# A graph and memory-lookup network on one core: the lookup's vector y kept in PSUM, score tiles copied to SBUF, the selection spread over half steps, and layer-2 products summed over two source tiles

## The reference

```python
x = x + gelu(batch_norm(gcn(LN(x)))) + LN(x)       # layer 1, graph
y = LN(x)                                          # layer 1, lookup
q = (y @ Wq + bq).reshape(-1, 8, 128)              # 8 heads, two halves of 64
s1, s2 = q[..., :64] @ keys1.T, q[..., 64:] @ keys2.T      # 256 scores each
t1, i1 = top_k(s1, 8); t2, i2 = top_k(s2, 8)
best8, pos = top_k(all 64 sums t1[a] + t2[b], 8)
rows = i1[pos // 8] * 256 + i2[pos % 8]            # 64 rows of 65536 per node
inner = sum_d y[d] * w_down[rows, d]
x = x + sum_rows relu(inner) * softmax(best8) * w_up[rows]
x = x + (segment_sum(LN(x)*deg_out**-.5)[src] -> dst) * deg_in**-.5 @ W + b   # layer 2, graph
x = x + LN(x) @ W[bin(LN(x)[0])]                   # layer 2, one of 8 experts
```

## Time and profile before

| | µs |
|---|---|
| median of three runs | 1503.99 |
| the profiled execution, its own time | 1505.18 |
| its span, first to last instruction | 1503.4 |
| first gather issued | 369.1 |
| lookup result added: tile 0, tile 8, tile 9 | 501.35, 1269.47, 1350.38 |
| mean granted TensorE clock, share of full | 0.934 |

### The profile page before, as it was taken

One profiled execution on the slowest core, in us unless ns is written; L12 is line 12 of the kernel. 1 busy time (PEld: TensorE's weight loads), 2 busy tenths in 40 slices (PEclk: granted clock), 3 DMA queues, 4 the chain that ended last, 5 costly groups with the idle time before them and its releaser, 6 DMA issues.

```text
span 1503.4 us, 15734 instructions
## 1 busy us (share of the span) xinstructions
PE 1208.2 (80%) x3844; PEld 576.9 (38%) x3845; DVE 988.0 (66%) x2819; ACT 431.9 (29%) x1128; POOL 710.4 (47%) x706
## 2 busy tenths in 40 slices
PE   2887889975789789778887898788989897689387
PEld 1343345543434244343342443434435342234133
DVE  3778791126587977949859689497795985565411
ACT  1767610023323232322322323123232232220010
POOL 2000000001676676756767767576676677643212
PEclk9999999986798999989999999899999999899689
DMA  8200000001998999989989999899999999977343
GB/s 351 114 0 1 1 1 0 0 0 36 352 341 294 350 364 326 361 318 329 357 308 359 374 330 348 319 346 376 326 365 354 334 365 360 375 280 255 128 162 114
DMA packets 105763, 378.73 MB, mean 252 GB/s; under 512 B 11824, under 2 KB 11826, under 8 KB 104536
## 3 DMA queue, kind: packets, MB, share of 16 engines
q0 software_dynamic: 94720, 343.40, 62.0%
q1 hardware_dynamic: 10968, 34.48, 6.2%
HBM read 359.53 MB, written 19.41 MB: 252 GB/s over the span
## 4 chain that ended last, share of the span: by engine, by line
PE 44%; DVE 29%; issue 10%; DVEq 4%; another core or an unknown queue 4%; DMA 3%; ACT 3%; POOL 3%; ACTq 0%; POOLq 0%; SPq 0%
PE tr L1288 16%; DVE big L991 12%; PE acc L1190 6%; PE acc L1162 5%; PE acc L1248 4%; DVE topi L885 4%; PE acc L1266 4%; DVE top L882 3%; PE tr L1337 3%; PE tr L1313 2%; PE acc L1220 2%; POOL big L473 2%; DVE outT L876 1%; DVE outT L739 1%
## 5 line engine op out<-in xcount | busy, mean ns | idle before, releaser
L473 POOL DMA_INDIRECT big<-in_wdu,idx x640 | 664.7, 1039 | 666.3 <-DVE idx L930 359.2
L1288 PE MATMUL tr<-big,diag 128*128 128x512 f32 x1280 | 626.9, 620 | 123.2 <-ACT diag L643 66.0
L991 DVE CUSTOM_DVE_ANT_0 big<-big,y,prob 128x512 f32<-128x512 f32 x640 | 450.1, 746 | 59.3 <-DMA big<-in_wdu,idx 39.1
L1288 PEld LDWEIGHTS tr<-big,diag 128*128 128x128 f32 x1280 | 234.4, 194 | 436.6 <-issue 323.7
L643 ACT ACTIVATE diag<-ident,inner 128x128 f32<-128x128 f32 x640 | 219.4, 393 | 491.3 <-DVE inner L991 270.9
L1162 PE MATMUL acc<-outT 128*128 128x512 f16 (+1 forms) x612 | 129.4, 370 | 29.5 <-DVE outT L739 22.7
L1266 PE MATMUL acc<-AT,gt 128*128 128x512 f32 (+1 forms) x240 | 109.6, 543 | 23.8 <-DVE outT L876 13.4
L882 DVE MAX8 top<-acc 128x8 f32<-128x256 f32 x160 | 60.9, 422 | 99.5 <-PE acc L1258 50.8
L739 DVE TENSOR_SCALAR outT<-big 128x1280 f16<-128x1280 f16 x204 | 102.6, 549 | 35.2 <-PE acc L1162 33.4
L876 DVE TENSOR_TENSOR outT<-outT,acc 128x512 f32<-128x512 f32 (+1 forms) x120 | 69.9, 584 | 67.6 <-remote 45.2
L1248 PEld LDWEIGHTS acc<-yT,qk 128*128 128x128 f32 x640 | 87.4, 213 | 34.4 <-issue 33.3
(11 more groups left out here) (212 smaller groups left out, 735.0 us busy)
## 6 DMA issues: line engine op xcount, KB each, us to landing
sorted_rows<-big SPq DMA_DIRECT2D x8, 1280.0 KB, 17.3
big<-in_wdu,idx POOLq DMA_INDIRECT x640
big<-in_we SPq DMA_DIRECT2D x8, 1024.0 KB, 13.9
x<-sorted_rows SPq DMA_DIRECT2D x14, 512.5 KB, 3.4
x<-in_x SPq DMA_DIRECT2D x1, 2304.0 KB
qk<-in_wq SPq DMA_DIRECT2D x1, 2048.0 KB, 19.8
big<-in_w0t SPq DMA_DIRECT2D x1, 1024.0 KB, 27.2
qk<-in_keys SPq DMA_DIRECT2D x1, 1024.0 KB, 19.6
```

Of the source, the lines that this page charges most:

```text
L473: pool.indirect_dma_start(out=k.big[:, slot * 2 * D:(slot + 1) * 2 * D], out_offset=None, in_=k.wdu_d, in_offset=bass.IndirectOffsetOnAxis ...
L991: ins = dve.tensor_tensor_reduce(out=k.big[:, slot:slot + D], in0=k.big[:, slot:slot + D], in1=k.y[:, (i % 3) * D:(i % 3 + 1) * D], scale= ...
L1288: ins = pe.matmul(k.O[i % 2], k.diag[:, c:c + P], k.big[:, slot:slot + D], start=(g == 0 and s == 0), stop=(g == NG - 1 and s == GS - 1))
```

## The change

- **y.** VectorE computes only the factor and the offset (y_inv, two small operations); ScalarE applies them (y_norm, 128x512) into one SBUF tile, which TensorE transposes, and shortly before the tile's lookup copies it into a PSUM bank (keep_y; k.Y, two banks). The dots read y from there. Before each tile VectorE waits for `y_kept`. x_norm of layer 2 goes to ScalarE in the same way, into three h1 tiles.
- **Scores.** TensorE writes both halves of a head into one buffer of two banks; ScalarE copies them to SBUF in one instruction (copy_scores); MAX8 and FIND_INDEX8 read there. TensorE waits for ScalarE's copy of the head before. ScalarE's copy waits until the head before the last is selected. qT holds 4 heads.
- **Places.** The search of a tile starts 26 groups ahead of the one before it and takes 3 groups per head; MAX8 and FIND_INDEX8 are steps of their own (maxes, finds), and so is `sums`, taken out of best. Tile 1 has its own table. The tables below give, in this order, the places of y_stats, y_root, y_inv, y_norm, y_flip, y_copy, y_keep, the four queries, the eight scores, s_copy, maxes, finds and sums; q_copy is one place behind its query, and best, place, codes, match, rows and index follow sums one by one, softmax 8 behind it.
- **Units.** Source tiles (0,1), (2,3), (4,5), (6,7) are multiplied together: two products accumulate in the bank, then one addition; tiles 8 and 9 stay single. A unit comes every 5 groups (single ones every group). The first pair's results are copied into agg1, so the memsets go. The self-loops are subtracted before the batch norm.

```diff
-Y_STATS, Y_NORM = -14, -11
-HEADS = (-4, -3, -1, 0, 2, 3, 5, 6)
-BEST, PLACE, CODES, MATCH, ROWS, INDEX, SOFTMAX = 8, 9, 10, 11, 12, 13, 15
-Y_ROOT, Y_FLIP, Y_COPY = -13, -10, -9
-QUERIES = (-9, -7, -5, -3)
-Q_COPY = (-8, -6, -4, -2)
-SCORES = (-6, -5, -3, -2, 0, 1, 3, 4)
-X_ADD, X_STATS, X_ROOT, X_NORM = 4, 5, 6, 7
-UNIT_MM = [8 + 2 * u for u in range(NU)]
-UNIT_ADD = [11 + 2 * u for u in range(NU)]
+STEADY = Places(-26, -25, -23, -22, -21, -20, 2, (-19, -16, -9, -3), [3 * h - 15 for h in range(H)],
+                [3 * h - 13 for h in range(H)], [3 * h - 9 for h in range(H)], [3 * h - 8 for h in range(H)], 14)
+FIRST = Places(-6, -5, -4, -3, -2, -1, 1, (0, 2, 6, 8), [2 * h + 2 for h in range(H)],
+               [2 * h + 3 for h in range(H)], [2 * h + 4 for h in range(H)], [2 * h + 4 for h in range(H)], 19)
+X_ADD, X_STATS, X_ROOT, X_INV, X_NORM = 5, 8, 9, 11, 12
+UNIT_TILES = [(0, 1), (2, 3), (4, 5), (6, 7), (8,), (9,)]
+PAIRED, AHEAD = 4, 4
+for p_ in range(PAIRED):
+    for u_ in range(NU):
+        if p_ < PAIRED - 1 or u_ < AHEAD:
+            m_, a_ = (2 * p_ + 2) * NG + 14 + 5 * u_, 5
+        else:
+            m_, a_ = (NT - 1) * NG + 2 * (u_ - AHEAD), 3
+for u_ in range(NU):
+    m_ = (NT - 1) * NG + 16 + u_
...
+    def y_norm(i):
+        act.wait_ge(k.yco_ready, i + 1)
+        act.activation(k.y[:, :], k.x[:, i * D:(i + 1) * D], ACT.Identity, bias=k.yco[:, 1:2],
+                       scale=k.yco[:, 0:1]).then_inc(k.y_ready, 1)
+    def keep_y(i):
+        act.wait_ge(k.y_ready, i + 1)
+        if i >= 2:
+            act.wait_ge(k.inner_ready, (i - 1) * NG)
+        act.activation(k.Y[i % 2], k.y[:, :], copy).then_inc(k.y_kept, 1)
+    def copy_scores(i, h):
+        act.wait_ge(k.s_ready, i * H + h + 1)
+        if i * H + h >= 2:
+            act.wait_ge(k.topk_done, i * H + h - 1)
+        act.activation(k.sc[h % 2].rearrange("p (c n) -> p c n", c=2), k.S[:, :, 0:NK], copy).then_inc(k.sc_ready, 1)
...
-            dve.max(k.top[:, c * HK + h * 8:c * HK + h * 8 + 8], k.S[h % 2][c][:, 0:NK])
+            dve.max(k.top[:, c * HK + h * 8:c * HK + h * 8 + 8], k.sc[h % 2][:, c * NK:(c + 1) * NK])
...
-                    in1=k.y[:, (i % 3) * D:(i % 3 + 1) * D],
+                    out=k.big[:, slot:slot + D], in0=k.big[:, slot:slot + D], in1=k.Y[i % 2],
...
-        pe.wait_ge(k.topk_done, max(i * H + h - 1, 0))
+            pe.wait_ge(k.sc_ready, i * H + h)
...
+        for j in tiles:
+            ins = pe.matmul(k.G[n % 2 if n >= TWO_BANKS else 0][:, 0:cols], k.h1[j % 3][:, f * P:(f + 1) * P],
+                            k.AT[:, j * NPAD + c0:j * NPAD + c0 + cols], start=(j == tiles[0]), stop=(j == tiles[-1]))
```

More of the change, by code:

```diff
@@ L63, with __init__ @@
 NU = len(UNITS)
[L66 to L84 removed]
+class Places:
+    def __init__(self, y_stats, y_root, y_inv, y_norm, y_flip, y_copy, y_keep, queries, scores, s_copy, maxes, finds,
+                 sums):
+        self.y_stats, self.y_root, self.y_inv, self.y_norm = y_stats, y_root, y_inv, y_norm
+        self.y_flip, self.y_copy, self.y_keep = y_flip, y_copy, y_keep
+        self.queries, self.scores, self.s_copy, self.maxes, self.finds = queries, scores, s_copy, maxes, finds
+        self.q_copy = [q + 1 for q in queries]
+        self.sums, self.best, self.place, self.codes = sums, sums + 1, sums + 2, sums + 3
+        self.match, self.rows, self.index, self.exps, self.softmax = sums + 4, sums + 5, sums + 6, sums + 5, sums + 8
@@ L619, in exps, with search_step @@
         act.activation(k.ex[:, :], k.sm[:, :], ACT.Exp).then_inc(k.exp_done, 1)
-    def search_step(i, at):
-        if at == Y_ROOT:
+    def search_step(i, at, g):
+        if g == at.y_root:
             y_root(i)
-        if at == Y_COPY:
+        if g == at.y_norm:
+            y_norm(i)
+        if g == at.y_copy:
             copy_yT(i)
-        if at in Q_COPY:
-            copy_q(i, Q_COPY.index(at))
-        if at == EXPS:
+        if g == at.y_keep:
+            keep_y(i)
+        if g in at.q_copy:
+            copy_q(i, at.q_copy.index(g))
+        if g in at.s_copy:
+            copy_scores(i, at.s_copy.index(g))
+        if g == at.exps:
             exps(i)
@@ L634, in tile @@
                 x_root(i - 1)
-            for j, at in at_search(i, g):
-                search_step(j, at)
+            if i and g == X_NORM:
+                x_norm(i - 1)
+            for j, at, place in at_search(i, g):
+                search_step(j, at, place)
             n = i * NG + g
@@ L647, in act_program @@
     gelu(0, 0)
[L648 to L649 removed]
+    for g in range(FIRST.y_root, FIRST.exps + 1):
+        search_step(0, FIRST, g)
     for i in range(1, NT):
         gelu(i, i % 2)
[L652 to L653 removed]
+    for g in range(FIRST.y_root, 0):
+        search_step(1, FIRST, g)
     for i in range(NT):
@@ L656, in act_program @@
     x_root(NT - 1)
+    x_norm(NT - 1)
     with act.Fori(0, NT) as t:
@@ L807, in dve_program @@
                           ALU.mult).then_inc(k.aggT_done, 1)
+    for t in range(NT):
+        loops = k.AT[:, t * NPAD + t * P:t * NPAD + (t + 1) * P]
+        dve.tensor_tensor(loops, loops, k.ident[:, :], ALU.subtract)
     dve.memset(k.outT[:, :].rearrange("p (o c) -> p o c", c=NPAD)[:, :, N:NPAD], 0.0)
@@ L996, in tile @@
             ins.then_inc(k.inner_ready, 1)
-    for at in range(Y_STATS, SOFTMAX + 1):
-        search_step(0, at)
+    for g in range(FIRST.y_stats, FIRST.softmax + 1):
+        search_step(0, FIRST, g)
     for i in range(1, NT):
@@ L1294, in pe_program @@
     pe.sem_inc(k.grp_done, RING)
-    for at in range(Y_FLIP, SCORES[-1] + 1):
-        search_step(0, at)
+    for g in range(FIRST.y_flip, FIRST.scores[-1] + 1):
+        search_step(0, FIRST, g)
     for i in range(1, NT):
@@ L1299, in pe_program @@
     pe.wait_ge(k.x1_done, NT)
+    for g in range(FIRST.y_flip, 0):
+        search_step(1, FIRST, g)
     for i in range(NT):
```

198 lines of the change are left out of this document (110 added, 88 removed).

## The result

The changed kernel took **1511.26 µs** in the median of 20 runs (1501.94 to 1523.88), the kernel before, beside it, 1504.26 (1489.77 to 1517.17). The ratio is **1.0065, 95% interval 1.0041 to 1.0089**: slower by 0.65%, about the 0.5% that can be told, where 1429 was forecast. The profiled execution took 1506.09, its span 1504.0. On one the kernel before takes 1487 to 1504 and the changed one, where it was run, is slower; on the other the kernel before takes 1418 and the changed one is **3% faster**. The trace tells which kind it is. "Chip" is short for chip, host and moment together, which the runs don't tell apart: the chip that has number 15 in its host was of both kinds, in different runs.

A forecast was written before the change was run, and what follows sets the result against it. No engine was full and all were near it, with a DMA floor of 83.2 µs per 96.0 µs tile. Terms of -68, -11, +1, +1 and +0.5 gave -76.5 from 1505.2, so 1429 µs, range 1395 to 1474.

The forecast's parts named there:

- near 0.94: GpSimd's gathers in the lookup: expected to fall to about 0.94 µs each once dots read y from PSUM.
- rival C: Lookup dots: reading y from PSUM is slower and VectorE becomes the bound; 1520 to 1675 µs, chance 0.06.
- The 65 ns more: Lookup dots: the skill page's estimate of extra cost per dot reading PSUM, 4.1 µs of VectorE per tile; forecast took none.
- Tile 0: Lookup's first tile, 114.4 µs from first dot to result: forecast 103, so -11 µs (bounds -3 and -16).
- The stretch ahead of the first dot: Serial first search before the lookup: ScalarE's longer norm and a score copy add 1 µs (0 to 2).
- the last tile: End of the lookup: 28 unit products instead of 12 just fit TensorE, +1 µs (-2 to +5).
- the first term: Lookup tiles 1 to 8: 87.5 µs each instead of 96.0, -68 µs in all (bounds -96 and -32).
- the 86.2 of the tile with half a search: Window from tile 8's result: 12 units, half a search, 86.2 µs at full clock; the base for an ordinary tile's 87.5.
- The 1.3: Tiles 1 to 8: 1.3 µs per tile added for late completions and half clock that the gather ring doesn't cover.
- rival A: Lookup tiles: TensorE's late completions still stop everything; tiles 92 to 96 µs, kernel 1474 to 1508, chance 0.09.
- the lock step: Lookup search after a late completion: engines hand on one step at a time, costing 9 µs, expected mostly gone.
- rival B: Lookup tiles: everything hides, no lock step, GpSimd undisturbed, tiles at the DMA's 83.2 µs; kernel 1388, chance 0.07.

The follow-up runs named there:

- x5: The changed kernel, unedited, run again on a chip with late updates: ratio 1.0113 to the kernel before.
- z2: The changed kernel with its search steps back at the old, bunched places, on a chip with late updates: 1537.8 µs, 3.6% slower than the kernel before.
- z1: The changed kernel with ScalarE's query copies 4 groups behind their products from tile 3 on, search started earlier, late updates: 1477.2 µs, ratio 0.9928 to the kernel before.
- x1: The changed kernel with its search steps back at the old, bunched places, where no update is late: 1397.9 µs, the kernel before taking 1418.4.
- w1: The changed kernel with all of ScalarE's search copies 3 or 4 groups behind their products, on a prompt chip: ratio 0.9697 to the kernel before.

## Why the prediction was wrong

**What held.** VectorE 69.6 per tile for 69.4 forecast; gathers 949 ns for "near 0.94"; dots 742 ns where they had been 746, no price for PSUM, so rival C falls. The 65 ns more of the estimate by the Trainium skill's fixed cost (VectorE: DVE Perf Modes, TRN2 errata) would have shown and aren't there. There are 72 additions or copies of units (60 are in the row above). ScalarE has 31.4 for 33.9.

**The sum against the trace.** Tiles 1 to 8 gave +4.2 µs for -68. Tile 0, 108.9 µs from its first dot (384.7) to its result for 114.4, gave -5.5 where -11 was forecast, and its result is now added one group later. The stretch ahead of the first dot gave -2.3 for +1, the last tile +2 for +1 (82.9 for 80.9), the stretch after it +2.2 for +0.5 (155.2 for 153.0). Together +0.6 for -76.5: the first term is nearly all of the miss. (Two slips of the working change nothing: its bounds add up to 1391 and 1479, not 1392 and 1474, and rival C at d = 0.45 comes to 1527, not 1520.)

**The step that failed** is that first term: "the 86.2 of the tile with half a search, plus 1.3 for late completions and half clock that the ring doesn't cover". The 1.3 took the late completions to be a cost of about one stop per tile that the spread places would absorb. The trace shows 96.5 for 87.5. That is rival A in its mechanism, and just above its prices (tiles of 92 to 96, 1474 to 1508). The argument against A was the error: "the DMA ran at full rate through the stop itself" is true (405 GB/s in the stop above) but buys nothing, since the ring then stands full, TensorE has its groups still to do, and the mean over the tiles is 347. The granted clock fell too, 0.94 for 0.97.

**Why more stops.** In the kernel before the steps of a search lay close together, and one stop covered several. With the steps 3 groups apart ScalarE goes and stands in line for TensorE at many separate places. Its waits named "remote" in front of the qT copies went from 5 to 11 times (43.7 to 80.1 µs in the three traces of the kernel before) to 21 (206.9) and, in x5, 17 (172.1); late updates from 38, 47 and 56 to 92 and 95. Stretches of over 4 µs in which an update hung, in tiles 1 to 8, went from 9 and twice 12 to 26 and 25. That the places set this number is shown by z2, which has 11. But the time doesn't follow the number: z2 is the slowest of all, and z1, with 31 such stretches, is the fastest on its kind of chip. How much of the 9 µs a tile each part costs stays open, and so does what makes an update late. I had weighed the distances against VectorE's waits and not against ScalarE's, where each copy of the queries stood one group behind its product with all diagonals queued behind it; that this is part of the cost is what z1 makes likely.

**The other error was taking one trace for the kernel.** The kernel before, unedited, takes 86 µs less where no update is late (1418 for 1504), more than the whole -76.5: much of what the sum wanted to win from the lock step was the price of late updates. Where none is late the changed kernel has 83.5 per tile and 1377 in all. That isn't the forecast but rival B: it lies under the forecast's lower bounds (84 and 1392), and the argument against B, that TensorE would have to be busy over 90% with clock drops, met 93% (622.34 of 668.0) at a granted clock of 1.00. The gain is 41 µs only because the kernel before has 1418 there. The tile of the trace at 86.2 was taken for an ordinary one less its troubles; it was a nearly undisturbed one (three late updates, of 2.1 to 2.4 µs).

## What to carry to other kernels

If an engine stands in line for another's result with unrelated work behind it, try its place several groups behind the product, not one: that cost nothing where all was prompt (0.9712 for 0.9707 on one chip), and where updates came late it went with 1.4 to 1.8% less, by ratios from different chips. A stop that recurs in a trace without a cause is a term of its own: count how many places of the new order can catch it before taking it as covered. And measure a change on more than one chip: here its sign depended on it.

## What was not expected of the hardware

On some chips TensorE's semaphore updates come up to 12.3 µs late (x5) while gathers are in flight, and at the end of a stop several follow 0.06 µs apart; on others none of the 387 to 445 in a trace is over 0.02 late. The traces with late ones have 4874 to 6143 landing records for 11303, and VectorE's instructions dribble. The late updates are real, since ScalarE starts 0.02 µs after one. Late updates and lost records come together in all seven traces that have either, and in none of the other thirteen. A guess that would fit, and that nothing here tests: engine events and their recording share a path that falls behind on some machines. The Trainium skill (NOTIFIC — the notification-queue block, 7.1 Overflow) has it that the block's internal pipeline holds its producers back rather than lose a record, so recording can throttle an engine; no run here shows that this is the cause, and the lost records speak against that rule alone. Every execution here was profiled, so the time without recording isn't known. Nor does the number of the chip in its host tell the kind: number 15 was prompt in x1 and w1 and late in z1.
